# Quantised weights as one byte per element instead of four, in a pre-norm block with gated projections and a quantised FFN on eight cores

## The reference

```python
# sublayer 1 (its input is _layernorm(x); inside, it is normalised again, with gamma and beta)
projected = jnp.einsum('bsd,ed->bse', xn, W_in)          # W_in 8192 x 2048
z, gate = jnp.split(projected, 2, axis=-1)
output = z * sigmoid(clip(z)) * softmax(-dt) * silu(clip(gate))
output = jnp.einsum('bse,de->bsd', output, W_out)        # W_out 2048 x 4096
# sublayer 2: 5632 hidden units; W = (wq - 128) * scale, wq int32 with values 0 to 255
gate = silu(_qlinear(x, wq_gate, s_gate))
up   = _qlinear(x, wq_up, s_up)
return _qlinear(gate * up, wq_down, s_down)
```

## Time and profile before

| | |
|---|---|
| median of the runs | 7908.91 us (7907.16 to 7910.66, 2 runs) |
| the profiled execution | 7866.47 us |
| its span on the slowest core (core 7) | 7864.9 us |
| spans of the 8 cores | 7824.1 to 7864.9 us |
| mean granted clock of TensorE over the span | 0.92 |
| TensorE busy (matmuls) | 6749.6 us, 86% |
| VectorE, ScalarE, GpSimd busy | 1908.8, 1235.0, 337.1 us |
| moved by DMA | 1627.88 MB, 207 GB/s on the mean |

### The profile page before, as it was taken

One profiled execution on the slowest core, in us unless ns is written; L12 is line 12 of the kernel. 1 busy time (PEld: TensorE's weight loads), 2 busy tenths in 40 slices (PEclk: granted clock), 3 DMA queues, 4 the chain that ended last, 5 costly groups with the idle time before them and its releaser, 6 DMA issues.

```text
span 7864.9 us, 84815 instructions; the slowest of 8 cores (7824.1 to 7864.9 us)
## 1 busy us (share of the span) xinstructions
PE 6749.6 (86%) x30208; PEld 2982.1 (38%) x30208; DVE 1908.8 (24%) x3342; ACT 1235.0 (16%) x1572; POOL 337.1 (4%) x630
## 2 busy tenths in 40 slices
PE   3557555699899998999899989999899989999898
PEld 1222222244344443444344434444344434444343
DVE  3332211214211421114211431123211430123210
ACT  2111323111110202111110211111210211111210
POOL 1110112100000000000000000000000000000000
PEclk9778777799899999999899999999899999999899
DMA  5887788884547563574548563575448464665447
GB/s 191 278 272 248 260 272 305 284 271 158 187 152 259 181 222 123 186 255 168 179 152 267 172 217 129 196 245 179 164 153 280 162 206 139 205 215 187 159 152 249
DMA packets 409690, 1627.88 MB, mean 207 GB/s; under 512 B 46544, under 2 KB 46640, under 8 KB 375872
## 3 DMA queue, kind: packets, MB, share of 16 engines
q1 hardware_dynamic: 328320, 1195.52, 45.5%
q0 software_dynamic: 80960, 426.95, 16.4%
HBM read 1469.18 MB, written 153.11 MB: 206 GB/s over the span
## 4 chain that ended last, share of the span: by engine, by line
PE 74%; DMA 14%; DVE 5%; ACT 3%; issue 3%; POOL 0%; DVEq 0%; POOLq 0%; ACTq 0%; SPq 0%
PE pb L375 74%; DMA wu_s<-wb 3%; DMA wg_s<-wb 2%; DMA wd_s<-qo 2%; DMA win_s<-wb 2%; ACT xnT L672 1%; DVE bnb L531 1%; DMA qi<-winT 1%; DMA xb<-woutT 1%; DMA out<-gsc 1%; DMA qi<-woutT 1%; DVE xres L587 1%; DMA wout_s<-qo 1%; DVE gsc L626 0%; DMA xb<-winT 0%
## 5 line engine op out<-in xcount | busy, mean ns | idle before, releaser
L375 PE MATMUL pb<-xnT,wb 128*128 128x512 bf16 x19456 | 4397.2, 390 | 583.8 <-DVE actb L609 322.0
L375 PEld LDWEIGHTS pb<-xnT,wb 128*128 128x128 bf16 x19456 | 1940.3, 100 | 3037.0 <-issue 870.8
L375 PE MATMUL pb<-wb,actb 128*128 128x512 bf16 x9728 | 2186.5, 386 | 177.6 <-DVE gsc L626 60.2
L375 PEld LDWEIGHTS pb<-wb,actb 128*128 128x128 bf16 x9728 | 962.4, 99 | 1400.4 <-issue 302.2
L609 DVE SCALAR_TENSOR_TENSOR actb<-pb,suct,gsc 128x512 bf16<-128x512 f32 x352 | 264.2, 751 | 2029.9 <-PE pb L375 2025.0
L726 ACT ACTIVATE gsc<-pb,sgct 128x512 f32<-128x512 f32 x352 | 241.9, 687 | 1878.1 <-PE pb L375 1873.8
L375 PE MATMUL pb<-idmt,xn 128*128 128x128 bf16 x1024 | 167.1, 289 | 335.7 <-ACT xn L703 118.6
L682 ACT ACTIVATE gsc<-gsc 128x512 f32<-128x512 f32 x256 | 161.1, 629 | 1185.9 <-DVE gsc L570 1183.0
L325 POOL DMA_DIRECT2D out<-gsc x128 | 69.1, 540 | 6236.1 <-DVE gsc L626 6214.5
L570 DVE TENSOR_SCALAR gsc<-pb 128x512 f32<-128x512 f32 x256 | 177.1, 692 | 591.2 <-PE pb L375 587.6
L573 DVE TENSOR_TENSOR gsc<-gsc 128x512 f32<-128x512 f32 x256 | 177.3, 692 | 413.5 <-ACT gsc L684 413.5
(11 more groups left out here) (90 smaller groups left out, 1241.4 us busy)
## 6 DMA issues: line engine op xcount, KB each, us to landing
wb<-wd_s SPq DMA_DIRECT2D x704, 512.0 KB, 5.3
wb<-wout_s SPq DMA_DIRECT2D x512, 512.0 KB, 4.8
wb<-win_s SPq DMA_DIRECT2D x448, 512.0 KB, 3.7
wb<-wg_s SPq DMA_DIRECT2D x308, 512.0 KB, 3.8
wb<-wu_s SPq DMA_DIRECT2D x308, 512.0 KB, 3.9
qi<-winT POOLq DMA_DIRECT2D x32, 1024.0 KB, 8.9
xb<-winT POOLq DMA_DIRECT2D x32, 1024.0 KB, 8.6
win_s<-wb POOLq DMA_DIRECT2D x64, 512.0 KB, 4.9
```

The lines of the kernel that those rows point to most:

```text
L375: i = E.matmul(out_ap, lhsT, rhs, start=start, stop=stop) if E else None
```

## The change

The three quantised matrices are handed to the kernel as uint8, of which the values 0 to 255 are the low byte of the int32; the host takes it out before the launch. The loads of wg, wu and wd move 128 x 2048 bytes, into the first quarter of the same ring buffers. The conversions at L515, L517 and L649 read uint8 instead of int32. Everything else, among it each wait and the order on each queue, is the same.

```diff
--- before.py
+++ after.py
@@ -8,6 +8,7 @@
 F32 = mybir.dt.float32
 BF16 = mybir.dt.bfloat16
 I32 = mybir.dt.int32
+U8 = mybir.dt.uint8
 AF = mybir.ActivationFunctionType
 AX = mybir.AxisListType.X
 
@@ -74,9 +75,9 @@
     out_hbm = nc.dram_tensor("out", [TPC, D], F32, kind="ExternalOutput")
     winT = nc.dram_tensor("winT", [NE2, 128, D], F32, kind="ExternalInput")
     woutT = nc.dram_tensor("woutT", [4096, D], F32, kind="ExternalInput")
-    wqg = nc.dram_tensor("wqg", [NH, 128, D], I32, kind="ExternalInput")
-    wqu = nc.dram_tensor("wqu", [NH, 128, D], I32, kind="ExternalInput")
-    wqd = nc.dram_tensor("wqd", [H, D], I32, kind="ExternalInput")
+    wqg = nc.dram_tensor("wqg", [NH, 128, D], U8, kind="ExternalInput")
+    wqu = nc.dram_tensor("wqu", [NH, 128, D], U8, kind="ExternalInput")
+    wqd = nc.dram_tensor("wqd", [H, D], U8, kind="ExternalInput")
     sgc_in = nc.dram_tensor("sgc", [128, NH], F32, kind="ExternalInput")
     suc_in = nc.dram_tensor("suc", [128, NH], F32, kind="ExternalInput")
     gcc_in = nc.dram_tensor("gcc", [128, ND], F32, kind="ExternalInput")
@@ -134,6 +135,7 @@
         qi_f32 = [qi[0][:, :].bitcast(F32), qi[1][:, :].bitcast(F32)]
         ring_i32 = [qi[0][:, :], qi[1][:, :], xb2[:, :].bitcast(I32), xb3[:, :].bitcast(I32)]
         ring_f32 = [qi_f32[0], qi_f32[1], xb2[:, :], xb3[:, :]]
+        ring_u8 = [r.bitcast(U8)[:, 0:D] for r in ring_f32]
 
         def xslot(p, tc):
             if p % 2 == 0:
@@ -277,7 +279,7 @@
             dma("dt1", dt_row, dtr_in[:, :], label="dtin")
             def qld(i_):
                 kind = ITEMS[i_][0]
-                dst = ring_f32[i_ % 4] if kind in ("win", "wout") else ring_i32[i_ % 4]
+                dst = ring_f32[i_ % 4] if kind in ("win", "wout") else ring_u8[i_ % 4]
                 ii = E.dma_start(dst, item_src(i_)) if E else None
                 u.inc(f"qi{i_ % 4}", 16, f"qld:{i_}", ii)
 
@@ -512,9 +514,9 @@
                 if kind in ("win", "wout"):
                     op(lambda: E.tensor_copy(out_ap, ring_f32[i_ % 4]), f"wqts:{i_}")
                 elif kind in ("wg", "wu"):
-                    op(lambda: E.tensor_single_scalar(out_ap, ring_i32[i_ % 4], -128.0, OP.add), f"wqts:{i_}")
+                    op(lambda: E.tensor_single_scalar(out_ap, ring_u8[i_ % 4], -128.0, OP.add), f"wqts:{i_}")
                 else:
-                    op(lambda: E.scalar_tensor_tensor(out_ap, ring_i32[i_ % 4], -128.0,
+                    op(lambda: E.scalar_tensor_tensor(out_ap, ring_u8[i_ % 4], -128.0,
                                                       sdbt[:, :], OP.add, OP.mult), f"wqts:{i_}")
                 if p0_direct(kind):
                     u.alias(f"sl:{slab_of_item(i_)}", f"wqts:{i_}")
@@ -646,7 +648,7 @@
                         pk, px = slab_list(0)[g_ - NWB][0], slab_list(0)[g_ - NWB][1]
                         if p0_direct(pk):
                             u.wait(E, f"wqst:{item_of_slab(pk, px)}")
-                    op(lambda: E.activation(out_ap, ring_i32[i_ % 4], AF.Identity,
+                    op(lambda: E.activation(out_ap, ring_u8[i_ % 4], AF.Identity,
                                             bias=m128[:, 0:1], scale=1.0), f"wqts:{i_}")
                     u.alias(f"sl:{g_}", f"wqts:{i_}")
                 else:
@@ -794,9 +796,12 @@
 
     winT_h = np.ascontiguousarray(rowslab(Win.T, NE2)[ZIG])
     woutT_h = np.ascontiguousarray(Wout.T)
-    wqg_h = rowslab(wq_g.T, NH)
-    wqu_h = rowslab(wq_u.T, NH)
-    wqd_h = np.ascontiguousarray(wq_d.T)
+    def lowbyte(a):
+        return np.ascontiguousarray(a.view(np.uint8)[..., 0::4])
+
+    wqg_h = lowbyte(rowslab(wq_g.T, NH))
+    wqu_h = lowbyte(rowslab(wq_u.T, NH))
+    wqd_h = lowbyte(np.ascontiguousarray(wq_d.T))
     sgc_h = np.ascontiguousarray(s_g.reshape(NH, 128).T)
     suc_h = np.ascontiguousarray(s_u.reshape(NH, 128).T)
     gcc_h = np.ascontiguousarray(gamma.reshape(ND, 128).T)
```

## The result

The changed kernel is faster: its time is 0.9739 of the kernel before, 95% interval 0.9705 to 0.9772. On the 7908.9 us of before that is 7702 us (7676 to 7729). The profiled execution took 7667.8 us (before 7866.5), its slowest core is now core 1. In some executions of either kernel one die or both are granted a lower TensorE clock and take longer; times here are of the others, and where the profile of an experiment fell into such an execution, its rows are of a core with the clock of the rest, or only the loop is read from them.

The account below looks back on a forecast made before the run. Bound: pass 0's gate/up loop, a chain of 132 weight stores, one in flight, landings stretched by 1 MB loads. 712.4 - 127 x 4.0 = 204.4 plus 5 saves 209 us, from 7908.9 to 7700 us; range 7655 to 7785.

Parts of the forecast that it names:

- The bound and the period: Gate/up loop of pass 0: a chain of stores, one in flight, period falling from 5.61 to 4.0 us (3.7 to 4.39).
- the sum: Whole kernel: 204.4 us saved over 127 store periods plus 5 us at the loop's end, 209 us in all.
- The load landing: 256 KB weight loads on GpSimd's queue: taken to land in 4.0 us, where 1 MB loads take about 8.5 us.
- the equation: Store period in the gate/up loop: p = 3.7 + 0.56 x (0.53 + L - p), with L a load's landing.
- The rule cited there: DMAs on GpSimd's queue: about 2.0 us fixed plus bytes over 436 GB/s, 3.2 us for a 512 KB store.
- The conversions: ScalarE and VectorE in pass 0: uint8 input takes as long as int32, 2.00 and 2.29 us an item.
- The rival that ends slower: Gate/up loop: ScalarE slower on uint8, loop slows only past 8.0 us a conversion; 7991 us at 9.0; chance 0.03.
- The stores wait for no conversion: Gate/up loop: an item's load and conversion use 7.4 of 16 us, so stores still don't wait for conversions.
- The tail: After the 128th store, up to the down projection: the load falls from 8.85 to 4.0 us, 5 us less.
- the rival that saw TensorE stay at 1.2 GHz: Gate/up loop: TensorE becomes the bound at 13.8 us an `h`, 4.6 us a period, 7776 us; chance 0.06.
- Small loads that disturb more than their bytes say: Gate/up loop: half of the excess over 3.7 us stays, period 4.65 us, 7783 us; chance 0.12.
- Loads hidden anyway: Gate/up loop: loads don't slow the stores, so only the tail gains, 7904 us; chance 0.04.

## Why the prediction was right, point by point

**The bound and the period: right.** Forecast 4.0 us a period and 508 us for 127; measured 4.00 and 508.0. The time came out as 7702 for 7700 us. That they meet so closely is luck in part. The loop took 683 to 726 us on the eight cores before and 501 to 508 after, so that one and the same core gained between 178 and 225 us, 200 on the mean; and the profiled execution became 199 us shorter, not 209 as in the sum.

**The way to the 4.0 was less exact than the result.** The load landing was taken as 4.0 us and is 4.3. With that the equation gives 4.1 us from overlap alone; the measured median is 3.87, and with 64 KB loads 3.72, so at short loads an overlap costs less than the 0.56 us a microsecond that the long loads showed (at 512 KB it came near, 4.74 for 4.6). What the equation lacked are the long periods, those beside SyncE's loads of the down weights and those that coincide with packets of the instruction queue: the mean is 0.13 us above the median. So one term was too large and another was missing, and the two errors cancelled: that the sum met 4.00 is luck, the mechanism is not.

The rule cited there (the Trainium skill, DMA: Bandwidth & Descriptors, Anatomy of one DMA — SWDGE (gpsimd) path) fits the stores: its estimate of 3.2 us for 512 KB is what after shows, 3.2, with a floor of 3.0. For the loads it does not: its estimate for 256 KB is 2.6 us and the rows have 4.3, 64 KB still takes 3.6; each is issued 0.53 us behind a store on the same queue, and no run here shows one alone.

**The conversions: right.** A uint8 input costs what an int32 input did, on ScalarE (L651) and on VectorE in both forms (L519, L517); columns as in the earlier trace rows:

```profile
L651 ACT ACTIVATE wb<-qi,m 128x2048 bf16<-128x2048 uint8 x41 | 82.1, 2002 | 138.5 <-DMA qi<-wqg 104.1 <-DMA qi<-wqu 34.4
...
L519 DVE SCALAR_TENSOR_TENSOR qo<-qi,sdbt 128x2048 bf16<-128x2048 uint8 x22 | 50.4, 2293 | 180.2 <-DMA qi<-wqd 180.2
...
L517 DVE TENSOR_SCALAR wb<-xb 128x2048 bf16<-128x2048 uint8 x3 | 3.7, 1227 | 5.7 <-DMA xb<-wqu 4.2 <-DMA xb<-wqg 1.4
```

ScalarE's 2002 ns stand against 2001, and L519's 2293 against 2293. The rival that ends slower needed 8 us.

The Trainium skill (VectorE: DVE Perf Modes, What auto-detection actually checks) has VectorE take its two-port mode "if a single source and the destination are in SBUF with outermost non-unit dims both even or equal", and names no width of the input there. The 1227 ns of L517 with a uint8 input agree: the same instruction with int32 took as long, in this group of the kernel before:

```profile
L515 DVE TENSOR_SCALAR wb<-xb 128x2048 bf16<-128x2048 int32 x3 | 3.7, 1227 | 8.0 <-DMA xb<-wqg 5.4 <-DMA xb<-wqu 2.6
```

**The stores wait for no conversion: right, though the waits look otherwise.** The waits of the loop, as in the earlier trace rows:

```profile
PE pb L377 <- DVE actb L611: 143.9, 40, 8.0
...
POOL wd_s L305 <- DMA wu_s<-wb: 120.7, 41, 5.4
POOL wg_s L305 <- DMA wd_s<-qo: 119.7, 41, 4.3
...
POOL wu_s L305 <- DMA wg_s<-wb: 65.2, 22, 4.5
POOL wu_s L305 <- ACT wb L651: 52.5, 19, 3.4
```

The last line, 52.5 us for ScalarE where there were 23.0, seems to be the new wait that was feared. It is not. One such store is that of 1108.88 us, a wu item. Two conversions on ScalarE stand around it:

```profile
1099.67 2.00 ACT L651 ACTIVATE wb<-xb,m 128x2048 bf16<-128x2048 uint8 x1 [3.68 <-DMA xb<-wqu]
...
1106.22 2.00 ACT L651 ACTIVATE wb<-qi,m 128x2048 bf16<-128x2048 uint8 x1 [3.77 <-DMA qi<-wqg]
```

By the order of GpSimd's queue the wu slab stored at 1108.88 us is the one converted from 1099.67 us on, done by 1101.67 us. The conversion that ended at 1108.22 us, to which the wait is put down, is that of a later wg slab; it ended when the landing of the store before did (1105.19 + 3.02 us in the chain of waits). That loads with a period less of time cost nothing says the same.

**The tail: the mechanism right, the size wrong.** The load of 8.85 us was to take 4.0 and save 5 us. It took 6.46:

```profile
1304.10 6.46 DMA xb<-wqd
...
1314.20 9.20 PE pb L377 x32
...
1324.64 10.53 PE pb L377 x48
```

It is issued where SyncE's loads of the down weights are already under way (the long periods around 1294 us in the timeline above), and the last burst of TensorE took 9.20 us, 8.44 in the chain of before. The tail is 21.1 us instead of 22.7: 1.6 saved, not 5.

**TensorE: right.** Bursts of 32 matmuls, in the loop of after:

```profile
1105.38 7.07 PE L377 MATMUL pb<-xnT,wb 128*128 128x512 bf16 x32 [3.15 <-DVE actb L611]
1117.23 8.70 PE L377 MATMUL pb<-xnT,wb 128*128 128x512 bf16 x32 [4.78 <-DVE actb L611]
```

The mean granted clock over these two bursts is 1.00 and 0.81, over the one of 9.78 us before 0.72: 7.07 us is 32 matmuls at the upper level, 2.4 GHz, and in the others part of them run at the lower one. With shorter gaps ahead of the bursts (here 3.15 and 4.78 us, before 7.20) come more matmuls at 2.4 GHz, the opposite of the rival that saw TensorE stay at 1.2 GHz. And it still waits 143.9 us for `actf` in the loop, down from 315.2.

**The other rivals.** Small loads that disturb more than their bytes say: that would have been 4.65 us a period and it was 4.00, and 64 KB loads took the loop from 508 to 499 us only, so little disturbance was left. Loads hidden anyway: they were hidden as far as conversions go, and their size cost 204 us all the same.

## What to carry to other kernels

Where one queue holds loads and stores and waits for each store to land, the loads can cost time even though no store waits for them, as the 1024 KB loads did here: look at the landing of the store, not at the wait for the load. Fewer bytes help such a chain through the landing; a second transfer in flight helps it more, up to the point at which the engines are full, and there the bytes count again (4.8 to 4.9 us an item with int32, at a share of 1.00). With uint8 it came to 2.4 us, at a share of 0.96, where TensorE was nearly full too.

## What was not expected

A DMA share of 0.85 was no bound, and 0.59 hid one as strict: with two stores in flight the same engines went to 1.00 and 0.86. And taking ever more bytes away saves less than it seems: from 256 to 64 KB a load the store's landing fell only from 3.2 to 3.0 us, while from 1024 to 256 KB it had fallen from 4.9 to 3.2.
